# Moving the store of x2's rows from first to last in a step of the sync queue's attention schedule

## What is computed

```python
def xattn(q, k, v, gamma):          # q = layernorm(x), k = v = ctx, 8 heads of 64 rows
    qk = einsum('bhdq,bhdl->bhql', qh, kh) * scale
    sm = softmax(qk, axis=-1)
    return gamma * einsum('bhql,bhdl->bhdq', sm, vh)
x = x + xattn(layernorm(x), ctx, ctx, gamma)      # this sum is x2
x = x + ffn(layernorm(x), ...)                    # router, 8 experts (top 2), a shared expert
```

## Time and profile before

| | us |
|---|---|
| median of 3 runs | 927.85 |
| lowest and highest | 922.9, 928.9 |
| the profiled execution | 931.65 |
| its span, first to last instruction | 929.9 |

### The profile page before, as it was taken

One profiled execution on the slowest core, in us unless ns is written; L12 is line 12 of the kernel. 1 busy time (PEld: TensorE's weight loads), 2 busy tenths in 40 slices (PEclk: granted clock), 3 DMA queues, 4 the chain that ended last, 5 costly groups with the idle time before them and its releaser, 6 DMA issues.

```text
span 929.9 us, 13754 instructions
## 1 busy us (share of the span) xinstructions
PE 863.5 (93%) x4624; PEld 715.8 (77%) x4624; DVE 570.5 (61%) x819; ACT 505.5 (54%) x862; POOL 442.8 (48%) x422
## 2 busy tenths in 40 slices
PE   4988898988986999999999999999999999999993
PEld 3666666666665888888888888888889999999992
DVE  4987888888762553442121212113989999999991
ACT  3886788778754332112111111112778888888881
POOL 5464666677450000004333000000589999999983
PEclk9998999999997999999999999999999999999996
DMA  9112223133234331400032002553945343434442
GB/s 104 47 35 86 85 80 135 57 113 113 80 125 136 103 102 46 136 1 1 2 136 25 1 0 91 187 187 105 336 103 91 69 89 69 83 75 83 76 68 35
DMA packets 63236, 81.24 MB, mean 87 GB/s; under 512 B 15369, under 2 KB 34825, under 8 KB 63186
## 3 DMA queue, kind: packets, MB, share of 16 engines
q1 hardware_dynamic: 53426, 60.14, 21.2%
q0 software_dynamic: 9760, 20.49, 12.3%
HBM read 53.01 MB, written 27.60 MB: 87 GB/s over the span
## 4 chain that ended last, share of the span: by engine, by line
PE 74%; POOL 11%; issue 7%; DVE 3%; ACT 2%; DMA 2%; POOLq 0%; SPq 0%; DVEq 0%; ACTq 0%
PE scores L1359 9%; PE scores L1360 9%; PE scores L1361 9%; PE bank L1373 4%; PE bank L1374 4%; PE bank L1375 4%; PE scores L1224 3%; PE bank L1459 3%; PE bank L1460 3%; PE bank L1461 3%; PE scores L1435 3%; PE scores L1437 3%; PE scores L1436 3%; PE bank L1435 3%; PE bank L1437 2%
## 5 line engine op out<-in xcount | busy, mean ns | idle before, releaser
L1016 DVE TENSOR_TENSOR sg<-scores,sg 128x512 f32<-128x512 f32 x44 | 30.4, 692 | 218.4 <-PE scores L1361 202.6
L1359 PE MATMUL scores<-x_hl,wsp 128*128 128x512 f32 x352 | 138.1, 392 | 0.0
L1360 PE MATMUL scores<-x_hl,wsp 128*128 128x512 f32 x352 | 137.8, 391 | 0.0
L1361 PE MATMUL scores<-x_hl,wsp 128*128 128x512 f32 x352 | 137.5, 391 | 0.0
L615 POOL DMA_INDIRECT slot_rows<-msrc,posi x32 | 36.1, 1129 | 184.6 <-PE scores L1361 178.2
L630 POOL DMA_INDIRECT xg<-x_normed_rows,meta x39 | 39.3, 1007 | 160.0 <-PE scores L1383 141.7
L789 ACT ACTIVATE sg<-scores 128x512 f32<-128x512 f32 x44 | 26.3, 598 | 160.2 <-PE scores L1361 160.2
L936 DVE TENSOR_TENSOR ptl<-bank,pth 128x512 fp32r<-128x512 f32 x128 | 87.7, 686 | 27.2 <-ACT pth L690 26.7
L690 ACT ACTIVATE pth<-bank 128x512 fp32r<-128x512 f32 x128 | 76.7, 599 | 43.2 <-PE bank L1233 42.5
L684 ACT ACTIVATE pb<-scores,negmax 128x512 f32<-128x512 f32 x128 | 88.1, 694 | 13.0 <-DVE negmax L926 13.0
L796 ACT ACTIVATE hh<-sg 128x512 fp32r<-128x512 f32 x44 | 27.8, 632 | 115.9 <-DVE sg L1016 100.9
(11 more groups left out here) (175 smaller groups left out, 2235.4 us busy)
## 6 DMA issues: line engine op xcount, KB each, us to landing
wex<-in_L_ffn_w_gate SPq DMA_DIRECT2D x8, 704.0 KB, 4.3
wex<-in_L_ffn_w_up SPq DMA_DIRECT2D x8, 704.0 KB, 6.1
xb<-in_x SPq DMA_DIRECT2D x16, 256.0 KB, 3.5
cn<-in_ctx SPq DMA_DIRECT2D x16, 256.0 KB, 3.0
x_rows<-xb SPq DMA_DIRECT2D x16, 256.0 KB, 2.0
x_normed_rows<-x2n SPq DMA_DIRECT2D x16, 256.0 KB, 2.3
x_normed_transposed<-x2T SPq DMA_DIRECT2D x16, 256.0 KB, 3.2
x_hl<-x_normed_transposed SPq DMA_DIRECT2D x4, 1024.0 KB, 5.2
```

Of the source, the lines that this page charges most:

```text
L1359: te.matmul(bk[:, :], hi, xhi, start=(h == 0), stop=False)
L1360: te.matmul(bk[:, :], hi, xlo, start=False, stop=False)
L1361: ins = te.matmul(bk[:, :], lo, xhi, start=False, stop=(h == HC - 1))
```

## The change

In SP's `step(i)` the call `store_rows(i - 1)` moves from the first place behind `load_x(i + 4)`. Nothing else is changed: the same transfers are issued, with the same waits.

```diff
             def step(i):
-                if there(i - 1):
-                    store_rows(i - 1)
                 if there(i - 3):
                     store_normed(i - 3)
                 if there(i + 2):
                     paced(i - 1, 8)
                     load_values(i + 2)
                 if there(i - 3):
                     store_columns(i - 3)
                 if there(i + 4):
                     paced(i, 3)
                     load_x(i + 4)
+                if there(i - 1):
+                    store_rows(i - 1)
                 if i == 7:
                     load_block(0, 0)
```

## The result

| | before | changed |
|---|---|---|
| median, us | 925.38 (4 runs, 920.69 to 928.9) | 898.62 (4 runs, 898.22 to 898.97) |
| the profiled execution | 931.65 | 898.57 |
| its span | 929.9 | 896.8 |

The ratio of the changed kernel's runs to those of before is 0.9714, with a 95% interval from 0.9663 to 0.9765.

The account below looks back on a forecast made before the run. GpSimd's wait for the late context load bounded attention-stage periods; removing it leaves mostly TensorE-bound periods of 13.9 us. Period gains of 27.3 us less 2 make 25, so 927.85 becomes 903 us, range 898 to 912.

Parts of the forecast that it names:

- The cause: SP's queue: the `cn` load needs nothing of the residual but stands behind the x2 store; `kh` waits about 3.2 us.
- The loop of 12.4 us: GpSimd's loop per attention-stage period without the wait at `kh`: 15.66 - 3.25 = 12.4 us, below TensorE's 13.89.
- the sum: Gains added over the attention stage's 13 periods: 27.3 us, less 2 us, giving 25 us.
- What the moved store passes: SP's queue: one store, one load, `store_columns` and `load_x`, costed at nothing; the store still leaves at about the same time.
- Its cover: SP's queue: the 5.9 us between 113.37 and 119.3 and the gap after, said to hide the passed edits.
- TensorE's period: Attention stage: TensorE becomes the bound with 13.89 us of work a period, against 15.66 us before.
- The allowance: Attention stage: 2 us taken off the whole gain for small new waits on VectorE or ScalarE.
- rival A: Attention stage: new waits, transposes wait for `ptl`, periods settle at 14.5 us, time 907; chance 0.09.
- Steps 9 to 12: Two more GpSimd instructions add some 1.9 us; GpSimd's loop of 14.3 us remains the bound in these four periods.
- The clock: TensorE's clock falls in three attention-stage periods, costing 7.2 us together, were expected to go with the waits for `x2n`.
- the case in which the falls stay: Attention stage: TensorE's clock falls stay or come elsewhere, time 903 + 7 = 910; chance 0.07.
- Rival B: SP's queue: nothing happens, the `cn` load is hidden anyway or something else holds it; time 928, chance 0.04.
- Rival C: Attention stage: slower, GpSimd's instructions collide with VectorE's, 4.9 us added to the loop, time 949; chance 0.03.

Follow-up runs that it names:

- first experiment: Kernel before with only the context load (`load_values`) taken ahead of the x2 store, which stays ahead of all other transfers: 897.42 us.
- third experiment: Changed kernel with one wait added, so the context load waits for the residual of tile i - 1: 909.43 us.
- fourth experiment: Changed kernel with the context load also waiting for the third transpose of tile i, leaving about 1.8 us before the residual's end: 897.66 us.
- seventh experiment: Changed kernel with the two GpSimd instructions of steps 9 to 12 moved from behind the residual to behind `kl`: 896.6 us.
- second experiment: Kernel before with the other two stores and the x load moved up, the x2 store last but one, the context load behind it: 913.42 us.
- second profile: The kernel before, unchanged, executed once more for another profile: 923.57 us.

## Why the prediction was right

The time predicted was 903, it is 898.62; the range of 898 to 912 holds it, near its low end.

**The cause** was as told. The load needed nothing of the residual and waited for it only through the queue. The first experiment shows it by giving the load its place without the rest, which brings the whole gain. The third puts the wait back without the order: of the 3.25 us of `kh` some 2.4 are the wait and some 0.8 the two issues ahead of the load. The load now leaves 0.03 us after the transpose that it waits for ends (99.84), as told, 7.4 us ahead of the residual's end where 8.1 were told. The loop of 12.4 us plus the wait of `kh`, on which the sum stood, holds in three kernels within 0.1 us.

**What the moved store passes** cost nothing, as costed: it still leaves 0.03 us behind the residual, as the queue's rows show. Its cover was misread by a little: the transpose of `e_t` = 8 i + 3 ends at 119.72 and not at 119.3, which makes it 6.35 us and not 5.9. The 7.7 us that were taken as the worst landing are those of a load issued at 15 us, ahead of all the periods; within them the slowest took 5.4.

**TensorE's period** is the term that was mis-sized. I took its busy time of the earlier trace rows, 13.89 us, as its work. Its work is 13.60 us: that is what it is busy in a period without a stall, in the changed kernel, in the fourth and in the seventh experiment. With two stalls in a period it is busy 13.89 (before) or 13.91 (second and third experiment), so that about 0.3 us of that came with the stalls and went with them. The rows show where it comes from. Before, the transposes of 110.03 run their full 0.66 us, and only then does the stall of 1.12 us in the earlier trace rows begin; in the changed kernel the next transposes start 0.50 us after these (TensorE's timeline):

```profile
97.84 0.66 PE L1233 MATMUL bank<-ident,pb 128*128 128x128 f32 x4
98.34 0.60 PE L1267 MATMUL bank<-ident,x2n 128*128 128x128 f32 x4
```

So, from start to start, the stall of 1.12 us delays TensorE by 1.28 (1.78 against 0.50): 0.16 us of a tail that otherwise lies under the next instruction is laid bare. At the second stall it is another 0.08. Over the 13 periods the sum had 181.7 us and they take 179.4: 2.3 us.

**The allowance** of 2 us for new waits was not needed. TensorE waits for `ptl` once in the 13 periods, 0.47 us in the first, which was forecast as bound by VectorE (13.4 us told, 13.45 found) and where it waited as long before; rival A asked for 14.5 us, and VectorE, at 13.06 of 13.60, still keeps up.

**Steps 9 to 12** were right: 14.3 predicted, 57.10 / 4 = 14.28 found, with a wait for `kl` of 0.6 us in each, 0.2 above the 0.4 predicted. The seventh experiment shows that it was the two instructions behind the residual.

**The clock** came out right for the changed kernel (1.00 in all 13 periods), and late loads were shown to cause falls. But the sum carried the three falls of one execution over to the median of the runs. One of them, 3.9 us, was not in the second profile, so for an execution like that one the periods are worth 29.6 - 3.9 = 25.7 us. That error ran against the two above and nearly made up for them, which was luck: 25 us predicted, 26.8 measured (925.38 to 898.62), 26.0 where both ran once more beside each other (923.99 to 898.01). Nor were the 7.2 us all the price of the clock. With the loop (12.4 us, and 14.3 in steps 9 to 12) and the wait of `kh` (5.65, 2.07 and 4.06 us) taken off the three periods (19.60, 17.2 and 17.39 us), 1.5, 0.9 and 0.9 us are left, 3.3 together; the rest was the longer wait for the load. So the case in which the falls stay was overpriced at 910. The other 2.5 us of the miss of 4.4 are the median of before, 927.85 of three runs and 925.38 of four. Between the two profiled executions, where nothing makes up for it, the forecast was 906.5 and the time 898.57: 2.3 us from TensorE's period, 2 from the allowance, 3.5 from outside the periods, the rest rounding.

**Rival B** fell with the first row of the queue. **Rival C** fell with the durations: `xb` 1.29 us, `kh` 0.61 us as before, with GpSimd 3 us earlier against VectorE. The Trainium skill (SBUF — State Buffer, on the shared port pair) gave the reason in advance, and the trace agrees as far as it goes: VectorE's two-input instructions on whole tiles in this stage (`ptl`, `vs`, `att`) each read `bank` in PSUM. Its BATCH_NORM_STATS2 reads `xb` in SBUF, against what the prediction says of the large instructions, but has that one input. No run here sets an instruction with two SBUF inputs against GpSimd, so the rule itself was not tested.

## What to carry to other kernels

Read an in-order DMA queue as you read an engine: for each load that is waited for, ask which of the waits ahead of it is its own. A store that waits for the end of a step belongs behind the loads that feed the next one, but here only the load's place counted, and only up to the point where another engine's work is longer than the loop: of the 7.4 us of head start won, the last 5.7 bought nothing (fourth experiment). When you forecast an engine-bound period, take the engine's busy time from a stretch without stalls; with stalls it is an upper bound.

## What the runs showed of the hardware that was not expected

- TensorE's granted clock fell, on an else undisturbed kernel, behind stalls of 1.77, 3.4 and 4.6 us, and not behind one of 1.61 us. Behind the normal stalls of before (1.1 and 0.6 us) it held at 1.00. The other profiles agree for the stalls at `x2n`: it fell behind each of 1.76 to 4.61 us, eight in all, to 0.50 to 0.67 over the next 4 us, and behind none of up to 1.65 us (second experiment). But a stall's length alone does not settle it. At the end of the stage TensorE stalls for 1.28 us and 4 us later for 0.91, in each of the fourteen profiles, and in four of them the clock fell behind that (to 0.72 to 0.78 over 4 us), in ten not. A fall adds 1.5 us to TensorE's busy time of a period behind the short stall (15.43 against 13.95) and 2.0 to 2.5 behind the long ones. The Trainium skill (TensorE: Matmul & The Clock Gate, Part 1) says that activity releases a throttle that is the default; the runs agree in direction.
- A stall costs more than its length: two stalls of 1.12 and 0.64 us lengthened a period of 13.60 to 15.66, by 2.06 and not 1.76 us. The excess does not follow their length: in the second and third experiment, with only 0.98 us of stalls in the period shown, TensorE's busy time is 13.91 us all the same.
- The load of 256 KB lands in 2.6 us (median of the changed kernel) where it is issued some microseconds away from the other transfers, in 3.0 us in the order of before, in the midst of three stores and another load. In the third and fourth experiment, where one store and a load follow it within 1 us, it is 2.9.
